# A graph-attention kernel's edge count: target one-hots moved from GpSimd to VectorE, in rings of nine, and the jobs between the counts dealt anew

## Chip, cores and metric

One core of a Trainium2 chip runs the whole program. The metric is the device time of one execution in microseconds (us), the median over the runs shown. Engines: TensorE (PE, its weight loads PEld), VectorE (DVE), ScalarE (ACT), GpSimd (POOL) and SyncE (SP), whose queue issues all DMAs here.

## What is computed

x is [1250, 512] in float32, with 20,000 edges (src, dst), sorted by dst. The reference, cut to what matters:

```python
h = layernorm(x)                                   # no gain
for l in range(2):                                 # 8 heads of 64
    q = (h @ Wq[l].T + bq[l]) * 64 ** -0.5; k = h @ Wk[l].T; v = h @ Wv[l].T
    scores = einsum('ehd,ehd->eh', q[dst], k[src])
    p = softmax of scores over the edges of one dst
    agg = segment_sum(p * v[src], dst)
    h = batchnorm(h + agg @ Wo[l].T + bo[l]) * g1[l] + beta1[l]
    h = batchnorm(h + relu(h @ W1[l].T + b1[l]) @ W2[l].T + b2[l]) * g2[l] + beta2[l]
x = x + layernorm(h) * ln_g + ln_b
x = x + ffn(layernorm(x))                          # nibble decode, three small MLPs, one-hots
```

The kernel computes the attention densely. Two nodes may be joined by several edges, so it needs a matrix of edge counts, count[dst, src]. It adds min(log(count), ...) to each score: the logarithm of the count where there is an edge, and -1e30 where there is none. This 1250 x 1250 matrix is called the bias; it is the same for both layers.

## The kernel before

Nodes are cut into ten tiles of 125 (`NT`, `TILES`). The first block of the program does three things at once, interleaved by hand: the edge count, the layer norm and transposition of the input, and the projections q, v and k of layer 0.

**Edge count.** For each tile j of targets, `counting(j)` on TensorE adds up products of one-hots in three PSUM banks (`counts`, banks 0 to 2): edges come in groups of 125 on the partitions, `onehot_dst[:, k, :]` (125 x 125) marks each edge's target in the tile, `onehot_src[:, k, :]` (125 x 1250) its source. One group takes three matmuls (512, 512 and 226 columns). A loop over registers runs over the groups that touch the tile; a table computed at the start holds first group, number of rounds and rounds before. One round is `RING` = 18 groups; VectorE makes the source one-hots (`step`, L745) into nine slots and the last three target one-hots of each 18, GpSimd makes the other fifteen (`targets`, L596), in steps of three (`STEP`). Then ScalarE computes relu and logarithm of the counts (`logs`), VectorE combines them in a minimum (`combine`, L770), and SP stores the row of the bias (`bias_out`). TensorE may begin the next count only after that minimum, since the banks are the same.

**Gaps.** Between two counts TensorE works through a gap. `GAP_TURNS` and `GAP_REDUCES` say which pairs of tiles of the normed input are transposed there (`turned`: 16 matmuls into two banks of 4 to 7) and split in a high part and a low part (ScalarE copies the high part, `less_high` on TensorE subtracts it, ScalarE copies the rest, `lower`). `JOBS[0]` lists the projection jobs, `GAP_ENDS` where each gap stops in the list, `BANKS[0]` the PSUM bank of each job: transposes of weights ("wq", "wv", "wk", four each; ScalarE and VectorE split them in two parts, `projected` and `reduced`), q and k products (twelve each, of 12 matmuls of up to 418 columns), v products (ten, of 12 matmuls of 512). The order in the list before is wq, q, wv, eight v, wk, two v, k.

```python
GAP_REDUCES = {1: (0, 1), 2: (2, 3), 3: (4,)}
GAP_TURNS = {0: (0, 1), 1: (2, 3), 2: (4,)}
GAP_ENDS = (1, 2, 4, 7, 11, 14, 20, 23, 26, len(JOBS[0]))
```

**Layer norm of the input.** ScalarE sums and squares the rows in two parts, of six and four tiles (`moments`, L632), VectorE finishes the scales after the count of tile 0, ScalarE norms the rows pair by pair. GpSimd adds ln_b to the input (`shift`, L194) for the residual at the very end, in two operations between its target one-hots.

**Keys.** Scores use a high and a low part of k stacked on the partitions, `k_stack`. ScalarE writes the high part to `k_hi`, VectorE the low part to `k_lo` (two buffers each), and `k_stacked` on SP copies both by DMA to where `k_stack` wants them: two DMAs for the high part and two for the low part per chunk c of 128 features. The buffers are reused for chunks 2 and 3. `first_bias` on SP loads the first three tiles of the bias for attention, after k_stacked(0).

The blocks after that: attention of layer 0 (20 passes of four units), output projection and feed-forward, the projections of layer 1 (which use `projected`, `reduced` and `k_stacked` too), attention and feed-forward again, and the final part.

## Time and profile before

| | us |
|---|---|
| runs | 1206.63, 1205.21, 1206.53 (median 1206.53) |
| the profiled execution | 1205.97 |
| its span (first to last instruction) | 1204.2 |
| busy in it: PE / PEld / DVE / ACT / POOL | 1061.8 / 881.6 / 745.8 / 582.0 / 438.1 |
| mean granted TensorE clock | 0.947 of 2.4 GHz |
| first block | 0 to about 299 |
| the ten counts end at | 34.47, 63.26, 92.54, 117.90, 143.60, 163.76, 181.36, 205.42, 224.58, 243.68 |
| last key product of layer 0 ends | 284.12 |
| attention of layer 0 begins | 299.03 |

The profile is of one execution. Busy time of an engine counts its instructions without waiting; a wait has its own column, with the instruction that ended it. PEclk is the clock that TensorE was granted in a stretch, as a share of 2.4 GHz. The counts' ends are the ends of `counting`'s last matmul (L836).

### The profile page before, as it was taken

The page shows a single profiled execution, that of the slowest core. Times are in us where ns is not written, and L with a number is a line of the kernel's source. Part 1 is how long each engine was busy: PE and PEld are TensorE (multiplying, and loading weights), DVE is VectorE, ACT ScalarE, POOL GpSimd, SP SyncE. Part 2 cuts the span into 40 slices and gives each one's busy share as a digit, 9 for nine tenths or more (in the row PEclk, how much of TensorE's full clock was granted, in tenths as well). Part 3 has the DMA queues.
Part 4 walks back from the last instruction along what each step waited for, and adds up shares of the span by engine and source line. Part 5 has one row for each costly group of instructions (what it writes and reads, how often), then busy time and mean ns, then how long its engine had stood idle before and what let it go on. Part 6 is the DMA issues. An engine that isn't in the chain of part 4 may idle for free. (4 is left out here: it accounts for less than half of the span.)

```text
span 1204.2 us, 19750 instructions
## 1 busy us (share of the span) xinstructions
PE 1061.8 (88%) x6706; PEld 881.6 (73%) x6706; DVE 745.8 (62%) x2360; ACT 582.0 (48%) x1085; POOL 438.1 (36%) x519
## 2 busy tenths in 40 slices
PE   3677898995999999999899499989999999989953
PEld 2455676785778888888698499777888888869842
DVE  5434664621767777777577521076777777757788
ACT  5433213231656666666524223365666666652445
POOL 5446665300434444444112100043444444411304
PEclk9878898998999999999999799999999999999985
DMA  6022230139841212123300452484121212321303
GB/s 135 22 90 73 70 114 25 39 71 216 201 101 35 57 35 56 36 47 108 105 1 22 135 117 55 98 193 106 35 56 36 56 35 46 110 79 23 68 2 86
DMA packets 52295, 90.27 MB, mean 75 GB/s; under 512 B 15714, under 2 KB 34014, under 8 KB 51944
## 3 DMA queue, kind: packets, MB, share of 16 engines
q1 hardware_dynamic: 52200, 89.04, 30.1%
q8 instruction: 55, 0.90, 0.3%
q14 instruction: 40, 0.33, 0.1%
HBM read 36.50 MB, written 21.61 MB: 48 GB/s over the span
## 5 line engine op out<-in xcount | busy, mean ns | idle before, releaser
L966 POOL TENSOR_SCALAR probs<-probs,mass_inv 125x1250 f32<-125x1250 f32 x160 | 211.0, 1319 | 359.1 <-DVE mass_inv L1091 359.1
L986 PE MATMUL banks<-k_stack,q_stack 128*125 128x416 f32 (+1 forms) x960 | 299.0, 398 | 19.4 <-DVEq L1069 14.0
L1082 DVE CUSTOM_DVE_ANT_0 probs<-banks,scores_bias 125x416 f32<-125x416 f32 (+1 forms) x480 | 267.3, 582 | 61.0 <-PE banks L986 56.6
L1000 PE MATMUL banks<-ident,probs 125*125 125x125 f32 x1600 | 259.9, 277 | 7.2 <-DVE probs_t L1073 5.2
L1000 PEld LDWEIGHTS banks<-ident,probs 125*125 125x125 f32 x1600 | 242.6, 188 | 30.2 <-issue 22.7
L1052 ACT ACTIVATE probs<-probs,neg_peak 125x1250 f32<-125x1250 f32 x160 | 213.4, 1334 | 53.4 <-DVE neg_peak L1105 53.4
L1041 ACT ACTIVATE probs_t<-banks 125x500 f32<-125x500 f32 x320 | 152.6, 478 | 115.6 <-PE banks L1000 115.4
L1015 PE MATMUL banks<-probs_t,v_pair 125*64 125x250 f32 x1600 | 186.2, 379 | 0.9 <-ACT probs_t L1041 0.9
L986 PEld LDWEIGHTS banks<-k_stack,q_stack 128*125 128x125 f32 x960 | 147.3, 192 | 47.7 <-issue 27.5
L1015 PEld LDWEIGHTS banks<-probs_t,v_pair 125*64 125x64 f32 x1600 | 107.4, 136 | 54.3 <-ACT probs_t L1041 1.3
L1073 DVE COPY probs_t<-banks 125x500 f32<-125x500 f32 x160 | 108.1, 676 | 56.6 <-PE banks L1000 56.6
L831 PE MATMUL banks<-onehot_src,onehot_dst 125*125 125x512 bf16 x540 | 111.1, 370 | 30.9 <-DVE onehot_src L754 24.9
L831 PEld LDWEIGHTS banks<-onehot_src,onehot_dst 125*125 125x125 bf16 x540 | 73.3, 150 | 68.7 <-issue 44.4
L754 DVE TENSOR_SCALAR onehot_src<-iota,e_col 125x1250 bf16<-125x1250 f16 x180 | 94.1, 588 | 38.3 <-PE banks L831 19.5
L611 POOL TENSOR_SCALAR onehot_dst<-own,target_col 125x125 bf16<-125x125 f16 x150 | 104.5, 714 | 10.2 <-POOL target_col L608 10.2
L332 PE MATMUL banks<-h_hi,wt_hi 128*128 128x416 f32 (+1 forms) x192 | 69.6, 362 | 10.0 <-DVE wt_lo L370 10.0
L675 ACT ACTIVATE more<-banks 125x1250 f32<-125x1250 f32 x10 | 12.2, 1216 | 124.0 <-PE banks L836 119.2
L332 PE MATMUL banks<-h_hi,wt_lo 128*128 128x416 f32 (+1 forms) x192 | 68.7, 358 | 0.0
L332 PE MATMUL banks<-h_lo,wt_hi 128*128 128x416 f32 (+1 forms) x192 | 68.7, 358 | 0.0
L1089 DVE TENSOR_SCALAR mass<-mass 125x1 f32<-125x1 f32 x160 | 24.6, 154 | 69.2 <-ACT probs L1052 69.2
L436 POOL CAST q_split<-q_t 128x250 fp32r<-128x250 f32 x40 | 15.8, 396 | 134.7 <-ACT q_t L351 79.1
L1133 POOL TENSOR_TENSOR h_lo<-t,h_hi 128x1250 fp32r<-128x1250 f32 x9 | 25.9, 2874 | 100.8 <-ACT h_hi L1268 100.8
(245 smaller groups left out, 1429.1 us busy)
## 6 DMA issues: line engine op xcount, KB each, us to landing
q_stack<-q_split SPq DMA_DIRECT2D x160, 125.0 KB, 2.3
scores_bias<-edge_bias SPq DMA_DIRECT2D x8, 1171.9 KB
edge_bias<-bias_row SPq DMA_DIRECT2D x10, 585.9 KB
k_stack<-k_hi SPq DMA_DIRECT2D x16, 312.5 KB, 5.4
k_stack<-k_lo SPq DMA_DIRECT2D x16, 312.5 KB, 5.7
resid<-residual SPq DMA_DIRECT2D x2, 2500.0 KB, 9.5
values<-v_stage SPq DMA_DIRECT2D x2, 2400.0 KB
residual<-t SPq DMA_DIRECT2D x4, 625.0 KB, 2.9
```

The costliest lines, as they stand in the source:

```text
L332: mm = nc.tensor.matmul(bank[:, 0:sn], w[:, i, c * P:(c + 1) * P], h[:, i, s0:s0 + sn], **edge)
L611: op = nc.gpsimd.tensor_scalar(onehot_dst[:, k, 0:NT], own[:, 0:NT], target_col[:, k:k + 1], None, ALU.is_equal)
L754: op = nc.vector.tensor_scalar(onehot_src[:, k % SLOTS_SRC, :], iota[:, :], e_col[:, 1, ds(first + RING * q + k, 1)], None, ALU.is_equal)
L831: last = nc.tensor.matmul(counts[:, s:s + w], onehot_dst[:, k, 0:NT], onehot_src[:, k % SLOTS_SRC, s:s + w], start=False, stop=True, skip_ ...
L966: nc.gpsimd.tensor_scalar(probs[:, u % 4, :], probs[:, u % 4, :], mass_inv[:, u % 4:u % 4 + 1], 1.0, ALU.mult, ALU.mult).then_inc(att["pro ...
L986: mm = nc.tensor.matmul(pb[0:NT, t % 5, 0:sn], q_stack[:, n % 2, half, part, tile * NT:(tile + 1) * NT], k_stack[:, head * N + s0:head * N ...
L1000: mm = nc.tensor.transpose(pb[0:NT, 5 + t % 2, j * NT:(j + 1) * NT], probs[:, u % 4, (j0 + j) * NT:(j0 + j + 1) * NT], ident[0:NT, 0:NT])
L1015: mm = nc.tensor.matmul(pb[half * DH:(half + 1) * DH, 7, 0:GN], v_pair[:, c % 2, j, half * DH:(half + 1) * DH], probs_t[:, n % 2, half, j, ...
L1041: nc.scalar.activation(to, of, ACT.Copy).then_inc(att["t_free0"], 1)
L1052: nc.scalar.activation(probs[:, u % 4, :], probs[:, u % 4, :], ACT.Exp, bias=neg_peak[:, u % 4:u % 4 + 1], accum_out=mass[:, u % 4:u % 4 + ...
L1073: nc.vector.tensor_copy(to, of).then_inc(att["t_free1"], 1)
L1082: nc.vector.tensor_tensor_reduce(out=probs[:, slot % 4, s0:s0 + sn], in0=pb[0:NT, t % 5, 0:sn], in1=scores_bias[:, (n % GROUPS) * GROUP + ...
```

## The change

- A round is nine groups (`STEPS` = 3), at least two rounds per tile. VectorE makes all one-hots: per step one operation for three target one-hots and three for source one-hots (`step`). GpSimd's `targets` is gone.
- VectorE makes the first round of a tile before it takes up the minimum of the tile before (`combine(j - 1)`) and the low parts of that gap (`reduces(j - 1)`); the other rounds follow in the loop.
- In tile 0 VectorE waits for all moments of the layer norm between the first round and the loop; one root and one scale operation serve all ten tiles. The input is loaded two tiles at a time.
- `shift` is done by VectorE, in tiles 3 and 4, between minimum and loop.
- ScalarE writes the high part of a key product into `k_stack` itself, in two halves of 64 partitions; VectorE writes the low part in two halves. Only the low part is copied by DMA. This holds for both layers.
- Jobs, gaps and banks are dealt anew: wq, ten q, wv, two q, ten v, wk, twelve k; all k products now come after tile 9's count, all else before it. SP's order follows: wv is loaded before wk, `first_bias` goes out before the last bias row is stored.

```diff
-STEPS = 6
+STEPS = 3
 RING = STEPS * STEP
-SLOTS_SRC = 9
-POOL_STEPS = 5
+LOADS_X = tuple(slice(i, i + 2) for i in range(0, TILES, 2))
...
-        JOBS = (turns("wq") + Q_JOBS + turns("wv") + V_JOBS[0:8] + turns("wk") + V_JOBS[8:] + K_JOBS,
+        Q_FIRST = [("q", c, n) for n in range(3) for c in range(DC)]
+        JOBS = (turns("wq") + Q_FIRST[:10] + turns("wv") + Q_FIRST[10:] + V_JOBS + turns("wk") + K_JOBS,
...
-        GAP_REDUCES = {1: (0, 1), 2: (2, 3), 3: (4,)}
-        GAP_TURNS = {0: (0, 1), 1: (2, 3), 2: (4,)}
-        GAP_ENDS = (1, 2, 4, 7, 11, 14, 20, 23, 26, len(JOBS[0]))
+        GAP_TURNS = {0: (0, 1), 1: (2,), 2: (3,), 3: (4,)}
+        GAP_REDUCES = {1: (0, 1), 2: (2,), 3: (3,), 4: (4,)}
+        GAP_ENDS = (1, 4, 7, 11, 18, 22, 25, 28, 34, len(JOBS[0]))
+
+        LOWER_FIRST = {2: 1, 5: 2, 6: 2, 8: 3, 11: 4}
...
             if job[0] == "k":
                 c, (s0, sn) = job[1], CHUNKS[job[2]]
-                if not job[2] and c >= 2:
-                    act.wait_ge(k_stored[c % 2], 64 * (c // 2))
...
-                nc.scalar.activation(k_hi[c % 2][:, s0:s0 + sn], bank[:, 0:sn], ACT.Copy).then_inc(proj["hi"], 1)
+                for half in range(2):
+                    own, s = slice(half * DH, half * DH + DH), (2 * c + half) * N + s0
+                    op = nc.scalar.activation(k_stack[own, s:s + sn], bank[own, 0:sn], ACT.Copy)
+                op.then_inc(proj["hi"], 1)
...
-                sp.dma_start(f32(k_stack[own, cols]), f32(k_hi[c % 2][own, :])).then_inc(k_stored[c % 2], 16)
                 sp.dma_start(f32(k_stack[other, cols]), f32(k_lo[c % 2][own, :])).then_inc(k_stored[c % 2], 16)
...
-                link(nc.vector.tensor_scalar(span[:, 1, :], span[:, 1, :], 8388608.0, None, ALU.subtract))
+                link(nc.vector.tensor_scalar(span[:, 1, :], span[:, 1, :], 8388608.0, 2.0, ALU.subtract, ALU.max))
...
+                def step(j, first, before, q, i):
+
+                    hold(dve, "dve", onehot_used, RING * (before + q) + STEP * (i + 1))
+                    ks, at_ = range(STEP * i, STEP * (i + 1)), first + RING * q + STEP * i
+                    own = iota[:, j * NT:(j + 1) * NT].rearrange("p (a n) -> p a n", a=1)
+                    targets = e_col[:, 0, ds(at_, STEP)].rearrange("p (k a) -> p k a", a=1)
+                    nc.vector.tensor_tensor(onehot_dst[:, ks.start:ks.stop, 0:NT], own.to_broadcast([NT, STEP, NT]),
+                                            targets.to_broadcast([NT, STEP, NT]), ALU.is_equal)
+                    for k in ks:
+                        op = nc.vector.tensor_scalar(onehot_src[:, k, :], iota[:, :], e_col[:, 1, ds(first + RING * q + k, 1)],
+                                                     None, ALU.is_equal)
+                    op.then_inc(onehots_ready, 1)
...
                 for j in range(TILES):
                     [(first, rounds, before)] = spans_of(dve, j)
-                    with dve.Fori(0, rounds) as q:
-                        for k in range(RING):
-                            step(j, first, before, q, k)
+                    for i in range(STEPS):
+                        step(j, first, before, 0, i)
                     if j == 0:
...
+                        variance()
+                    if j:
+                        combine(j - 1)
+                        reduces(j - 1)
+                    if j == 1:
                         scaled_bias(dve)
...
+                    if j in (3, 4):
+                        dve.wait_ge(shift_in, 16)
+                        dve.wait_ge(h_ready, TILES)
+                        shift(nc.vector, PARTS_X[4 - j]).then_inc(x_shifted, 1)
+                    with dve.Fori(1, rounds) as q:
+                        for i in range(STEPS):
+                            step(j, first, before, q, i)
+                    if j == 0:
+                        scale()
+                combine(TILES - 1)
+                reduces(TILES - 1)
```

`LOWER_FIRST` says which job must wait for which pair's lower copy, `TURN_AFTER` (not shown) which banks a transposition waits for. In `k_stacked` the semaphore counts 32 per chunk instead of 64.

How VectorE's order moves, at the end of tile 1's loop (L779 and L778 are its branches; L370 and L377 the low parts of weights; between L202 or L198 and the next one-hot the table is loaded to registers). Before:

```order
L779 REGISTER_ALU
L779 COMPARE_AND_BRANCH
L773 SCALAR_TENSOR_TENSOR bias_row<-banks,bias_row 125x1250
L370 TENSOR_TENSOR wt_lo_96<-banks,wt_hi_94 128x512
L202 TENSOR_LOAD table
L202 ISA x6
L204 REGISTER_ALU
L204 ISA
L205 ISA x2
L779 UNCONDITIONAL_BRANCH
L779 ISA
L754 ISA
```

After (first lines, and the end of the same round):

```order
L778 REGISTER_ALU
L778 COMPARE_AND_BRANCH
L198 TENSOR_LOAD table
L198 ISA x6
L200 REGISTER_ALU
```

```order
L736 TENSOR_SCALAR onehot_src<-iota,e_col 125x1250
L754 SCALAR_TENSOR_TENSOR bias_row<-banks,bias_row 125x1250
L377 TENSOR_TENSOR wt_lo_94<-banks,wt_hi_92 128x512 x3
L778 UNCONDITIONAL_BRANCH
L778 ISA
L733 ISA
L733 TENSOR_TENSOR onehot_dst<-iota,e_col 125x3x125
```

The minimum of tile 1 stood right behind the loop; now the table's load and nine pairs of one-hots of tile 2 stand ahead of it, and the branch into the loop behind it.

How SP's order moves at the end of the first block (L523 and L529 store a row of the bias, L448 and L454 are `stacked`, L399, L401 and L405, L407 are `first_bias`, L392 and L393 and after the change L399 `k_stacked`). Before, from the last row of the bias on:

```order
L523 DMA edge_bias<-bias_row 120x1250
L523 DMA edge_bias<-bias_row 5x1250
L448 DMA q_stack<-q_split 64x500 x8
L392 DMA k_stack<-k_hi_98 64x1250
L393 DMA k_stack<-k_lo_100 64x1250
L392 DMA k_stack<-k_hi_98 64x1250
L393 DMA k_stack<-k_lo_100 64x1250
L399 DMA scores_bias<-edge_bias 120x2x1250
L399 DMA scores_bias<-edge_bias 5x2x1250
L401 DMA scores_bias<-edge_bias 120x1250
L401 DMA scores_bias<-edge_bias 5x1250
L392 DMA k_stack<-k_hi_99 64x1250
```

After:

```order
L405 DMA scores_bias<-edge_bias 120x2x1250
L405 DMA scores_bias<-edge_bias 5x2x1250
L407 DMA scores_bias<-edge_bias 120x1250
L407 DMA scores_bias<-edge_bias 5x1250
L529 DMA edge_bias<-bias_row 120x1250
L529 DMA edge_bias<-bias_row 5x1250
L454 DMA q_stack<-q_split 64x500 x8
L399 DMA k_stack<-k_lo_96 64x1250 x2
L399 DMA k_stack<-k_lo_97 64x1250 x2
L399 DMA k_stack<-k_lo_96 64x1250 x2
L399 DMA k_stack<-k_lo_97 64x1250 x2
```

The bias load went from behind the first key chunk to ahead of the last bias row, and of sixteen key copies eight are left.

## Rows read from the trace of the kernel before

**Rows 1.** Stretches: us; busy PE, PEld, DVE, ACT, POOL; PEclk, DMA share, GB/s

```profile
34.47:45.96 11.49, 6.69 (x37) 6.55 (x37) 1.46 (x1) 9.46 (x13) 7.45 (x16) 0.70 0.21 57
...
188.15:205.42 17.27, 13.18 (x59) 8.51 (x59) 10.94 (x22) 0.59 (x2) 7.97 (x13) 0.80 0.04 15
...
233.06:243.68 10.62, 10.62 (x60) 7.16 (x59) 5.79 (x13) 0.87 (x2) 0.00 (x0) 1.00 0.01 2
243.68:284.12 40.44, 40.44 (x210) 37.54 (x209) 9.18 (x14) 12.59 (x23) 2.16 (x4) 1.00 0.55 124
284.12:299.03 14.91, 1.48 (x14) 1.12 (x13) 1.59 (x3) 1.47 (x4) 0.00 (x0) 0.71 0.96 211
```

**Rows 2.** Lines, 0 to 250 us: busy us, mean ns | idle before, releasers

```profile
L831 PE MATMUL banks<-onehot_src,onehot_dst 125*125 125x512 bf16 x540 | 111.1, 370 | 30.9 <-DVE onehot_src L754 24.9 <-POOL onehot_dst L611 6.0
...
L754 DVE TENSOR_SCALAR onehot_src<-iota,e_col 125x1250 bf16<-125x1250 f16 x180 | 94.1, 588 | 38.3 <-PE banks L831 19.5 <-issue 18.0
...
L773 DVE SCALAR_TENSOR_TENSOR bias_row<-banks,bias_row 125x1250 f32<-125x1250 f32 x10 | 14.6, 1459 | 53.6 <-ACT bias_row L679 53.6
...
L752 DVE TENSOR_TENSOR onehot_dst<-iota,e_col 125x375 bf16<-125x375 f16 x10 | 6.0, 603 | 0.3
```

**Rows 3.** Timeline (start us, us, engine, line) of PE, tiles 7 and 9

```profile
192.97 12.31 PE L831 MATMUL banks<-onehot_src,onehot_dst 125*125 125x512 bf16 x54 [4.08 <-DVE onehot_src L754]
...
233.73 9.81 PE L831 MATMUL banks<-onehot_src,onehot_dst 125*125 125x512 bf16 x54
```

**Rows 4.** Timeline, all engines, the end of the first block

```profile
292.13 1.34 ACT L346 ACTIVATE k_hi<-banks 128x418 fp32r<-128x418 f32 x3 [14.19 <-DMA k_stack<-k_lo]
292.68 1.59 DVE L367 TENSOR_TENSOR k_lo<-banks,k_hi 128x418 fp32r<-128x418 f32 x3 [14.12 <-ACT k_hi L346]
294.30 0.46 SPq L392 DMA_DIRECT2D k_stack<-k_hi  x1
...
297.11 1.00 SPq L393 DMA_DIRECT2D k_stack<-k_lo  x1
...
299.03 1.38 PE L986 MATMUL banks<-k_stack,q_stack 128*125 128x418 f32 x3 [13.43 <-DVEq L1069]
```

**Rows 5.** Timeline of DVE, first one-hots of tiles 2, 4 and 5

```profile
78.25 4.19 DVE L754 TENSOR_SCALAR onehot_src<-iota,e_col 125x1250 bf16<-125x1250 f16 x9 [3.13 <-issue]
...
123.57 6.15 DVE L754 TENSOR_SCALAR onehot_src<-iota,e_col 125x1250 bf16<-125x1250 f16 x1 [1.45 <-issue]
...
148.85 4.19 DVE L754 TENSOR_SCALAR onehot_src<-iota,e_col 125x1250 bf16<-125x1250 f16 x9 [1.13 <-issue]
```

**Rows 6.** Timeline of ScalarE at the start

```profile
13.85 0.63 ACT L637 ACTIVATE ln_scratch<-xs 125x512 f32<-125x512 f32 x1 [11.79 <-DMA xs<-in_x]
...
27.91 1.28 ACT L649 ACT_TABLE_LOAD   x1
```

**Rows 7.** Timeline of PE, pieces of the gaps

```profile
63.19 1.20 PE L858 MATMUL banks<-h_hi,minus_ident 128*128 128x250 f32 x8
...
66.89 5.46 PE L847 MATMUL banks<-ident,h_norm 125*128 125x125 f32 x32 [2.49 <-ACT h_lo L669]
...
227.39 0.39 PE L329 MATMUL banks<-wt_hi,h_hi 128*125 128x512 f32 x1
...
230.19 0.40 PE L329 MATMUL banks<-wt_hi,h_hi 128*125 128x512 f32 x1
...
249.30 1.91 PE L317 MATMUL banks<-ident,wk_nat 128*128 128x128 f32 x16
```

**Rows 8.** Line 1133 on VectorE: x count: ns min/median/max

```profile
L1133 DVE TENSOR_TENSOR h_lo<-t,h_hi x6: 803/806/810, 637.8 to 1120.5; 128x625 fp32r<-128x625 f32 x6
```

**Rows 9.** Timeline of POOL, tile 1 to tile 2

```profile
68.95 0.29 POOL L602 COPY own<-iota 125x125 f16 x1 [0.93 <-POOL onehot_dst L611]
```

**Rows 10.** Timeline of PE, first scores of pass 3, layers 0 and 1

```profile
339.96 0.65 PE L986 MATMUL banks<-k_stack,q_stack 128*125 128x418 f32 x2 [2.81 <-DMA q_stack<-q_split]
...
821.92 0.65 PE L986 MATMUL banks<-k_stack,q_stack 128*125 128x418 f32 x2 [2.50 <-DMA q_stack<-q_split]
```

More of the change, by code:

```diff
@@ L171, in gnn_ffn @@
         wk_in = sem("wk_in")
-        x_in = [sem("x_in0"), sem("x_in1")]
+        x_in = [sem(f"x_in{k}") for k in range(len(LOADS_X))]
         e_in, consts, e_float, e_turned, hits_ready, hits_turned = (sem(s) for s in (
@@ L355, in projected @@
                     act.wait_ge(res_stored, 16 * DC)
+                    if layer == 0:
+                        for k in range(2):
+                            act.wait_ge(shifted_stored[k], 32)
                 nc.scalar.activation(v_pair[:, :, job[1], :], bank[0:NT, 0:4 * DH].rearrange("p (c d) -> p c d", c=2), ACT.Copy)
@@ L366, in reduced @@
                 c, (s0, sn) = job[1], CHUNKS[job[2]]
-                op = nc.vector.tensor_tensor(k_lo[c % 2][:, s0:s0 + sn], bank[:, 0:sn], f32(k_hi[c % 2][:, s0:s0 + sn]), ALU.subtract)
+                if not job[2] and c >= 2:
+                    dve.wait_ge(k_stored[c % 2], 32 * (c // 2))
+                if not job[2] and layer == 0 and c < 2:
+                    for k in range(2):
+                        dve.wait_ge(bias_stored[k], 32 * (TILES // 2))
+                for half in range(2):
+                    own, s = slice(half * DH, half * DH + DH), (2 * c + half) * N + s0
+                    op = nc.vector.tensor_tensor(k_lo[c % 2][own, s0:s0 + sn], bank[own, 0:sn], f32(k_stack[own, s:s + sn]), ALU.subtract)
             else:
@@ L511, in _ @@
                 xv = x.rearrange("(t p) d -> p t d", p=NT)
-                for k, tiles in enumerate(PARTS_X):
+                for k, tiles in enumerate(LOADS_X):
                     for rows in SPREAD:
@@ L548, in _ @@
                 shifted(0)
[L549 to L552 removed]
+                turned_out("wv")
+                sp.dma_start(w_nat[0]["wk"][:, :, :], weight(gnn["Wk"], DC)[:, 0:DC, :]).then_inc(wk_in, 16)
+                for j in range(5, TILES - 1):
                     bias_out(j)
```

149 lines of the change are left out of this document (49 added, 100 removed).

## Prediction, made before the changed kernel ran

> **What bounds the kernel now.** On the page TensorE leads every other engine in busy time, so I looked for the stretches in which it idles or runs slowly. The table of stretches, cut at the beginning and end of each tile's count, gives them [rows 1]: a count that runs undisturbed takes 10.62 us (tile 9), the one of tile 7 takes 17.27 us at a mean clock of 0.80, the gap after tile 0 takes 11.49 us, and at the end of the block 14.91 us pass with 1.48 us of matmuls. The groups by line say what TensorE waits for in the counts [rows 2]: 24.9 us on source one-hots of VectorE, 6.0 us on target one-hots of GpSimd. VectorE meanwhile sat idle 53.6 us in front of its minimum with the logarithm (L773). The timeline of TensorE shows one such wait [rows 3]: in tile 7 the 54 matmuls start after 4.08 us of idling and take 12.31 us; in tile 9, started warm, they take 9.81. So a late first one-hot costs twice, in waiting and in half clock (1.2 of 2.4 GHz) behind it. At the end of the block [rows 4], ScalarE's copies of the keys' high parts waited 14.19 us for a DMA of the low parts to free the buffer, at a DMA share of 0.96 [rows 1]; SP issued its last copy at 297.11 and attention began at 299.03, 14.9 us behind the last projection matmul (284.12).
>
> **The change, part by part.** I build TensorE's time anew, from T, the end of a count.
> *One-hots.* GpSimd's part goes; VectorE makes six groups of three target one-hots per tile where it made one. Nine source one-hots take 4.19 us [rows 5], 0.465 from start to start where one alone lasts 588 ns; a group of three target one-hots lasts 603 ns [rows 2], by the same ratio 0.47. A step of three pairs is 3 x 0.465 + 0.47 = 1.87 us, nine pairs 5.6, a tile 11.2. TensorE uses three in 9.81 / 6 = 1.6 us. With nine ready when the count begins, TensorE has 4.9 us of work, and the second nine come in time if VectorE enters its loop by then.
> *The order.* VectorE's last one-hot of a tile ends about 2 us before T (TensorE still has the last three, 1.6), then 1.1 to 3.1 us pass in loading the table and entering (1.13 and 3.13 [rows 5]; 18.0 over ten tiles [rows 2]), nine pairs 5.6, the minimum 1.46: the bias row is ready at T - 2 + 1.7 + 5.6 + 1.5 = T + 6.8, where it used to follow the logarithm at once. TensorE's next count stands behind it, and that is hidden while a gap lasts over 6.8 us.
> *Layer norm of the input and tile 0.* ScalarE's sums began at 13.85 on the load of six tiles and its squares ended about 27.8, right ahead of the table load at 27.91 [rows 6]. With two-tile loads only the last two tiles of the first part wait for the full 13.85: 4 x 0.62 = 2.5 us earlier. But VectorE now waits for all of it between its first and second nine of tile 0: 25.3 + 0.2 + 0.9 to enter the loop + 5.6 = 32.0, and TensorE, idle for some 5.5 us once its first nine are used, does the last three by 33.8 at full clock or 35.3 at half. Before, tile 0 ended at 34.47 [rows 1]; I take 34.5, no gain. Which clock? The row that is nearest in length is the 4.08 us of idling in tile 7, which cost 2.5 us [rows 3]. The Trainium skill, TensorE: Matmul & The Clock Gate, What's actually happening, says that throttled is the default and activity releases it. By that rule it is 35.3 and 0.8 us more in all; the trace agrees where it can be read, with the clock of 0.80 in tile 7's count.
> *Gaps.* Prices [rows 7]: a v product 230.19 - 227.39 = 2.80 us, a weight's transpose 1.91 / 4 = 0.48; a k or q product from the gap after tile 9, which is four v, four transposes and twelve k in 40.44 us [rows 1], (40.44 - 11.2 - 1.9) / 12 = 2.28; the transposes of a pair of tiles 5.46 / 2 = 2.7, less_high of a pair 0.6; where a transpose needs a lower copy first, it begins at T + 3.6 (66.89 - 63.26). Gap 0 stays 11.5. Gap 1: 3.6 + 2.7 + 1.5 = 7.8. Gap 2: 0.6 + 2.7 + 3 products = 10.1. Gap 3: 0.6 + 2.7 + 4 products = 12.4. Gap 4: wait to 3.7 (bank 4 needs the last lower copy), 3 products, 4 transposes = 12.4. Gap 5: 2 q + 2 v = 10.1. Gaps 6 and 7: 8.4 each. Gap 8: 2 v + 4 transposes = 7.5. Sum of 1 to 8: 77.1. All exceed 6.8, the last one barely.
> *Stalls left.* Tile 1: VectorE's loop starts after the minimum and a weight's low part, 0.8. Tile 3: the shift waits for the last normed rows (I estimate 2.4 us into the count: a copy and two activations of ScalarE), runs, and only then the second nine come: 1.7. The shift itself: 806 ns for 625 elements [rows 8] gives at most 2.64 us for 2,048 and 3.96 for 3,072; the second is hidden in gap 3. The Trainium skill, VectorE: DVE Perf Modes, The TRN2 errata, has (N + 151) / 0.96 ns for such an add, 2.29 us for 2,048, which would make 1.7 into 1.4; for 625 it gives 808 ns, and the trace agrees with 806. With the shift off GpSimd goes its effect too: in tile 4 VectorE's first one-hot took 6.15 us beside it [rows 5].
> *Branch.* Each count now runs its loop body twice, so TensorE takes a backward branch that the trace of before never shows for it. Bounds: 0, since matmuls queued ahead cover it, and 0.93 us, GpSimd's idling at its own outer branch with a table load [rows 9]. I take 0.2 x 10 = 2.0, nearer to the covered end, for TensorE's forward branch is not visible at all.
> *Sum.* 34.5 + 11.5 + 9 x 10.62 + 2.5 + 77.1 + 12 x 2.28 + 2.0 = 250.5 for the end of the last key product (before 284.12).
> *Keys in place.* ScalarE and VectorE each do two half operations per product, about 0.9 + 1.1 us (1.34 / 3 and 1.59 / 3 each [rows 4]) under a product of 2.28: hidden, except behind the last. Half of the 16 key copies (312.5 KB each) go, and the first bias load now goes out during tile 9's count, so that no buffer is awaited. Then 2.0 + two issues of some 0.5 (0.46 at 294.30) + 0.9 to the next block (as 298.11 to 299.03): attention starts 4.0 us behind, at 254.5. The bias row of tile 9, the q stacks and four bank cycles lie in front of the key copies, but end some 13 us into 27 us of products.
> *After that* nothing is gained: the stall on q_stack was 2.81 us in layer 0 and 2.50 in layer 1 [rows 10], where the key copies had long landed, so it comes from bias and v traffic, which stays. Layer 1's projections keep TensorE full, so its halved copies gain nothing either.
> Total: 299.03 - 254.5 = 44.5 us. The profiled execution took 1205.97; that gives 1161.5, and against the median of 1206.53, 0.56 higher, 1162.
>
> **The rivals.**
> (a) *VectorE paces the tiles.* If both idlings (table, loop entry) are 3.1 us and one-hots take 0.54 as with some contention, the second nine begin to arrive at T - 1.4 + 3.1 + 6.8 + 1.5 + 3.1 + 2.3 = T + 15.4, where TensorE wants them at gap + 0.8 + 4.9, T + 13.2 to 14.1, and then at 2.3 us a step against 1.6: about 3.5 us in each of five tiles with short gaps, 17 in all: 1179. For it: VectorE's work per tile rises to some 15 us in one chain. Against: before, it kept pace with GpSimd contending.
> (b) *Better than forecast.* Branch free, tile 1 and 3 unstalled, x early enough for tile 0 to end at 33.5, the q_stack stall gone with the backlog: 2.0 + 2.5 + 1.0 + 2.8 = 8 us: 1154.
> (c) *The tail's stall stays*, since the low copies queue behind the bias loads: 10.8 us back, 1173. Against: half the bytes, and the bias load goes first by 20 us.
> (d) *Slower.* TensorE's backward branch in the middle of each count costs as much as VectorE's longest idling ahead of a first one-hot, 3.13 us [rows 5], with no matmul queued to cover it, and each such idling brings half clock behind it, 2.5 us as in tile 7 [rows 3]: 5.6 us a tile, 56 in ten, less the 2.0 that I have: 1216. It decides from (44.5 + 2.0) / 10 = 4.65 us a tile. Against: VectorE's idlings hold a table load too, GpSimd's own branch with one took 0.93 [rows 9], and TensorE entered its loops without a visible stop.
> (e) *The change doesn't do what it says*: a third round in a tile would add matmuls. 540 matmuls are 10 x 18 x 3 [rows 2], one round of 18 in every tile, so two rounds of nine are exactly as many. Excluded.
>
> **How the numbers follow.** Forecast 0.70, (a) 0.15, (b) 0.07, (c) 0.04, no gain at all 0.01, (d) 0.03. The forecast's own terms range over: branch 0 to 9.3 (+7.3), half clock behind the waits of gaps 1 and 4 (up to 2.5 each), tile 0 up to 2.5 later; not all together, 1154 to 1176. Taking in most of (b) and (c) and leaving out (d) and the worse half of (a): 1152 to 1178. A measurement of this kernel can tell 0.2% from no change: faster 0.96, same 0.01, slower 0.03.
>
> **What the new profile would show.** Counts of 10.6 to 11 us from tile 2 on, tile 3 near 12.3; one-hots at 0.465 us; no wait of TensorE on one-hots over 2 us but in tile 0; the minimum ending about 6.8 us after each count; the last key product ending near 250, attention starting some 4 us later, and no DMA wait on k_lo. Wrong would be: waits of the count's first matmuls on the bias row in every tile, waits in the middle of each count without a semaphore (the branch), or an end of the block beyond 270.

## The result, and the profile of the changed kernel

The changed kernel takes 1161.6 us (median of 4 runs, 1160.4 to 1162.6), the kernel before 1206.6 in the same session (4 runs, 1205.2 to 1208.1): a ratio of 0.963, 95% interval 0.961 to 0.964. The forecast was 1162.0. The last key product ends at 250.62 (forecast 250.5), attention starts at 255.12 (254.5), where before it started at 299.03 [rows 4]. From there on nothing was gained or lost that can be told: 905.7 us to the end of the span against 905.2. That remainder was 905.2 to 909.2 in the fourteen profiles of this study, which hides differences of a few us between medians; where an experiment acts on the first block, the start of attention is the sharper measure, and both are given.

Busy time on the page (busy, share of the span):

```profile
PE 1052.4 (91%) x6706; PEld 875.8 (75%) x6706; DVE 776.3 (67%) x2429; ACT 594.1 (51%) x1108; POOL 306.8 (26%) x306
```

VectorE took 30 us more and GpSimd 131 less than before. The groups by line, 0 to 260 us (no count runs after 223; busy us, mean ns, idle before), answer to [rows 2]:

```profile
L821 PE MATMUL banks<-onehot_src,onehot_dst 125*125 125x512 bf16 x540 | 103.4, 350 | 2.9 <-DVE onehot_src L736 2.7
...
L736 DVE TENSOR_SCALAR onehot_src<-iota,e_col 125x1250 bf16<-125x1250 f16 x180 | 87.3, 545 | 0.0
...
L733 DVE TENSOR_TENSOR onehot_dst<-iota,e_col 125x375 bf16<-125x375 f16 x60 | 32.9, 549 | 42.9 <-PE banks L821 38.0 <-issue 4.9
L754 DVE SCALAR_TENSOR_TENSOR bias_row<-banks,bias_row 125x1250 f32<-125x1250 f32 x10 | 14.6, 1458 | 4.9 <-ACT bias_row L662 4.9
```

TensorE's idling ahead of count matmuls fell from 30.9 to 2.9 us. VectorE waits for TensorE now (38.0 us, for free slots), and no more for the logarithm but in the last tile (4.9 of 53.6).

The stretches (us; busy PE, PEld, DVE, ACT, POOL; clock, DMA share, GB/s): gap 0, gap 4, count 5, count 8, twelve k products, end of the block:

```profile
31.57:44.38 12.81, 7.18 (x37) 6.96 (x37) 6.93 (x13) 10.36 (x15) 0.00 (x0) 0.73 0.18 49
117.68:133.61 15.93, 10.85 (x58) 10.21 (x57) 7.67 (x14) 7.28 (x11) 0.00 (x0) 0.89 0.51 137
133.61:145.89 12.28, 12.28 (x59) 8.05 (x59) 7.42 (x16) 0.00 (x0) 0.00 (x0) 0.86 0.23 86
194.40:205.02 10.62, 10.62 (x60) 7.16 (x59) 7.36 (x16) 0.87 (x2) 0.00 (x0) 1.00 0.02 5
223.07:250.62 27.55, 27.55 (x144) 26.93 (x144) 14.26 (x23) 13.73 (x24) 1.03 (x2) 1.00 0.59 145
250.62:255.12 4.50, 1.49 (x14) 1.13 (x13) 1.36 (x3) 1.16 (x3) 0.00 (x0) 0.89 0.23 49
```

The last line answers to the 14.91 us at a DMA share of 0.96 of [rows 1]. Gap 4 and the count behind it are the dear ones, and gap 0, at a clock of 0.73. The timeline (start, us, engine, line; idling in brackets) of the places that matter, in order of time:

```profile
6.98 0.63 ACT L620 ACTIVATE ln_scratch<-xs 125x512 f32<-125x512 f32 x1 [4.98 <-DMA xs<-in_x]
...
26.00 5.44 PE L821 MATMUL banks<-onehot_src,onehot_dst 125*125 125x512 bf16 x27 [1.60 <-DVE onehot_src L736]
...
36.38 6.73 PE L839 MATMUL banks<-ident,h_norm 125*128 125x125 f32 x32 [4.80 <-ACT h_norm L638]
...
59.13 1.45 DVE L754 SCALAR_TENSOR_TENSOR bias_row<-banks,bias_row 125x1250 f32<-125x1250 f32 x1
...
85.69 2.29 DVE L194 TENSOR_TENSOR xs<-xs,shift_all 125x2048 f32<-125x2048 f32 x1 [6.31 <-ACT h_norm L638]
...
100.21 3.36 DVE L194 TENSOR_TENSOR xs<-xs,shift_all 125x3072 f32<-125x3072 f32 x1
...
121.40 0.69 PE L331 MATMUL banks<-h_hi,wt_hi 128*128 128x416 f32 x1 [3.06 <-ACT h_lo L652]
...
133.61 0.73 PE L814 MATMUL banks<-minus_one,one_row 1*125 1x512 bf16 x3 [2.02 <-issue]
...
255.12 6.31 PE L978 MATMUL banks<-k_stack,q_stack 128*125 128x418 f32 x18 [3.01 <-DVEq L1061]
```

Counts 1 to 9 start at 44.38, 63.58, 83.89, 107.06, 133.61, 156.17, 175.27, 194.40 and 212.45; counts 0 to 9 end at 31.57, 55.01, 74.20, 95.54, 117.68, 145.89, 166.79, 185.89, 205.02 and 223.07. From these come the stretches used below. Every profile is of one execution, and some stretches differ between profiles although the edit leaves them alone: the end of tile 0 stood at 31.4 to 33.2 us in nine of them, gap 1 took 7.0 to 8.6 us without idle matmuls, and count 5 took 10.62 or 12.28. A difference of some 2 us in the start of attention can be no more than that.

### The profile page after: what moved, and what is told of

It is laid out like the page before. It is cut to its first block and busy times, and to the rows that moved or that the text cites. A ratio compares the mean times of both kernels' runs of the same rounds, so it can differ in the third digit from the quotient of the medians.

```text
span 1160.8 us, 19123 instructions
## 1 busy us (share of the span) xinstructions
PE 1052.4 (91%) x6706; PEld 875.8 (75%) x6706; DVE 776.3 (67%) x2429; ACT 594.1 (51%) x1108; POOL 306.8 (26%) x306
## 5 line engine op out<-in xcount | busy, mean ns | idle before, releaser
L1044 ACT ACTIVATE probs<-probs,neg_peak 125x1250 f32<-125x1250 f32 x160 | 213.4, 1334 | 53.7 <-DVE neg_peak L1097 53.6
L821 PE MATMUL banks<-onehot_src,onehot_dst 125*125 125x512 bf16 x540 | 103.4, 350 | 2.9 <-DVE onehot_src L736 2.7
L821 PEld LDWEIGHTS banks<-onehot_src,onehot_dst 125*125 125x125 bf16 x540 | 68.5, 141 | 37.4 <-issue 11.0
L736 DVE TENSOR_SCALAR onehot_src<-iota,e_col 125x1250 bf16<-125x1250 f16 x180 | 87.3, 545 | 0.0
L733 DVE TENSOR_TENSOR onehot_dst<-iota,e_col 125x375 bf16<-125x375 f16 x60 | 32.9, 549 | 42.9 <-PE banks L821 38.0
## 6 DMA issues: line engine op xcount, KB each, us to landing
resid<-residual SPq DMA_DIRECT2D x2, 2500.0 KB, 10.1
```

The costliest lines, as they stand in the source:

```text
L733: nc.vector.tensor_tensor(onehot_dst[:, ks.start:ks.stop, 0:NT], own.to_broadcast([NT, STEP, NT]), targets.to_broadcast([NT, STEP, NT]), A ...
L736: op = nc.vector.tensor_scalar(onehot_src[:, k, :], iota[:, :], e_col[:, 1, ds(first + RING * q + k, 1)], None, ALU.is_equal)
L821: last = nc.tensor.matmul(counts[:, s:s + w], onehot_dst[:, k, 0:NT], onehot_src[:, k, s:s + w], start=False, stop=True, skip_group_check= ...
L1044: nc.scalar.activation(probs[:, u % 4, :], probs[:, u % 4, :], ACT.Exp, bias=neg_peak[:, u % 4:u % 4 + 1], accum_out=mass[:, u % 4:u % 4 + ...
```

## Experiments

**1. Keys by DMA again.** In the changed kernel only this is undone, in both layers (the two high buffers, the waits for them and SP's copies of them, cut here, come back with it):

```diff
-                for half in range(2):
-                    own, s = slice(half * DH, half * DH + DH), (2 * c + half) * N + s0
-                    op = nc.scalar.activation(k_stack[own, s:s + sn], bank[own, 0:sn], ACT.Copy)
-                op.then_inc(proj["hi"], 1)
...
+                nc.scalar.activation(k_hi[c % 2][:, s0:s0 + sn], bank[:, 0:sn], ACT.Copy).then_inc(proj["hi"], 1)
...
+                sp.dma_start(f32(k_stack[own, cols]), f32(k_hi[c % 2][own, :])).then_inc(k_stored[c % 2], 16)
```

> The changed kernel (1161.6 us) with one part undone: the keys' high parts go through two buffers and DMAs again, with the waits that the kernel before had for them (ScalarE before chunk 2, SP at the end of both blocks); the order of jobs, the one-hots and the early bias load stay as changed. Theory A (the tail's gain has two sources: half the key copies and no buffer to wait for, and the bias load moved ahead of all key copies): the high copy of chunk 2 waits for chunk 0's four DMAs, which start only behind the q stacks (about 237 us in), so some 2 to 4 us of TensorE's pauses come back, and SP issues 8 more copies (0.5 to 2 us each) ahead of the next block: attention starts 3 to 7 us later than 255.1, total 1165 to 1169, expected 1167. Theory B (keys in place is the whole gain of the tail): attention starts 14.9 us behind the last key product again, total about 1172 or more. Theory C (the order of the bias load is the whole gain): within 1.5 us of the changed kernel.

Measured: 1166.0 us (1162.9 to 1170.5). Its timeline at the end of the block:

```profile
246.40 1.34 ACT L346 ACTIVATE k_hi<-banks 128x418 fp32r<-128x418 f32 x3 [8.04 <-DMA k_stack<-k_lo]
...
256.46 1.62 SPq L396 DMA_DIRECT2D k_stack<-k_lo  x1
...
260.13 6.09 PE L977 MATMUL banks<-k_stack,q_stack 128*125 128x418 f32 x18 [7.21 <-DVEq L1060]
```

The last key product ended at 251.44, so 8.7 us pass to the start of attention, where the changed kernel has 4.5; attention starts 5.0 us later in all. Theory A holds, in one detail not as told: ScalarE waited 8.04 us for the copies, but TensorE's products took 27.55 us as before, without a pause. The price comes only at the end, from copies that SP issues late (its last at 256.46).

**2. The bias load behind the key copies.** The changed kernel with SP's old order:

```diff
-                first_bias(sp)
...
                 bias_out(TILES - 1)
                 for n in range(2):
                     stacked(sp, n)
-                for c in range(DC):
+                k_stacked(sp, 0, 0)
+                sp.wait_ge(proj["copied"], len(V_JOBS) + len(Q_JOBS))
...
+                first_bias(sp)
+                for c in range(1, DC):
                     k_stacked(sp, 0, c)
```

> The changed kernel with SP's old order at the end of the block: the first bias load (four DMAs, 1.9 MB) stands behind the last bias row, the q stacks and the key copies of chunk 0, so it goes out near 239 us instead of 214; keys stay in place. Theory A (two sources of the tail's gain): the copies of chunks 1 to 3 land behind these 1.9 MB, VectorE's low part of chunk 3 waits some 4 us for its buffer and the end of the block moves by 2 to 4 us: expected 1164, range 1163 to 1166. In the kernel before with keys in place the attention started 7.2 us behind the last key product, 2.7 more than the 4.5 here. Theory B (keys in place is the whole gain): 1161 to 1162.3. Theory C (the order is nearly the whole): 1168 or more.

Measured: 1168.3 us (1163.6 to 1172.1), 11.4 us between last product (248.36) and attention, which starts 4.7 us later than in the changed kernel.

```profile
236.28 2.14 SPq L405 DMA_DIRECT2D scores_bias<-edge_bias  x2
...
254.09 3.64 DVE L374 TENSOR_TENSOR k_lo<-banks,k_stack 64x418 fp32r<-64x418 f32 x6 [10.16 <-DMA k_stack<-k_lo]
```

The mechanism is theory A's, but I had priced the wait at 4 us and it is 10.16: the copies of chunk 1 go out behind 1.9 MB and hold the buffer of chunk 3. In size it is theory C's case, above theory A's range.

**3. Keys in place alone**, in the kernel before (the inverse of the first diff, one-hots, jobs and SP's order as they were).

> The kernel before (1206.5 us) with one part of the change alone: the keys' high parts are written in place by ScalarE in two halves, only the low parts are copied by DMA, in both layers. One-hots, jobs and SP's order stay as before (the bias load behind the key copies of chunk 0). Theory A (two sources, see the other experiment): ScalarE waits no more, VectorE's low parts of chunks 2 and 3 still wait for copies that stand behind the first bias load; attention starts 5 to 9 us earlier than at 299.0: 1198 to 1202, expected 1199. Theory B (keys in place is all of the tail's gain, 10.4 us): 1196. Theory C (the order is all): 1205 to 1207.

Measured: 1197.1 us (1195.4 to 1198.8), ratio to before 0.9925 (0.990 to 0.995).

```profile
283.12 3.64 DVE L371 TENSOR_TENSOR k_lo<-banks,k_stack 64x418 fp32r<-64x418 f32 x6 [5.93 <-DMA k_stack<-k_lo]
...
288.82 2.42 PE L989 MATMUL banks<-k_stack,q_stack 128*125 128x418 f32 x6 [5.71 <-DVEq L1072]
```

By the total this misses theory A's range (1198 to 1202) and stands nearer to B's 1196. The stretch itself says otherwise: 7.2 us from the last product (281.62) to attention, against 14.9, so in place alone gives 7.7 of the 10.4 us. The other 2.5 us came before the last product, where the edit touches nothing until the key products (the longest piece is count 2, 18.07 us against 19.82). With experiments 1 and 2: 14.9 with neither, 8.7 with the order alone, 7.2 or 11.4 with keys in place alone (in the kernel before, in the changed one), 4.5 with both. No single edit is the whole gain of the tail, so theory B falls, by experiments 1 and 2 above all. The two also save partly the same time.

**4. VectorE not ahead.** The changed kernel, with the minimum and the low parts in front of the first round:

```diff
+                    if j:
+                        combine(j - 1)
+                        reduces(j - 1)
                     for i in range(STEPS):
                         step(j, first, before, 0, i)
                     if j == 0:
                         variance()
-                    if j:
-                        combine(j - 1)
-                        reduces(j - 1)
```

> The changed kernel with one part undone: VectorE takes up the minimum and the low parts of the gap before the first round of one-hots, instead of after it. All else stays, also that VectorE makes all one-hots. Theory A (being ahead is what removes the waits): the bias row comes 1.4 us earlier, which nobody waits for, but in the gaps with weight transposes (0, 1, 4 and 8) VectorE can begin one-hots only when the last low part is written, about 2 us behind the gap's end, so those counts begin 2 to 3 us late and then go at VectorE's pace (1.83 us a step against 1.6) at half clock for a while, 3 to 5 us each, 12 to 20 in all; in the other tiles the nine are ready or nearly. Expected 1176, range 1171 to 1183. Theory B (it was GpSimd's slow target one-hots alone, the order of VectorE's work is worth nothing): 1160 to 1164.

Measured: 1179.1 us (1177.3 to 1180.9), attention at 271.13, 16.0 later. The count matmuls by line, then stretches (counts 1, 2, 4, 5 and 9):

```profile
L821 PE MATMUL banks<-onehot_src,onehot_dst 125*125 125x512 bf16 x540 | 109.2, 364 | 15.1 <-DVE onehot_src L736 14.9
```

```profile
42.38:58.28 15.90, 12.32 (x59) 8.04 (x59) 11.71 (x26) 3.01 (x6) 0.00 (x0) 0.89 0.01 2
65.32:81.97 16.65, 12.75 (x59) 8.32 (x59) 13.03 (x27) 3.11 (x6) 0.00 (x0) 0.79 0.32 102
...
115.39:126.01 10.62, 10.62 (x59) 7.16 (x59) 6.35 (x13) 0.14 (x1) 0.00 (x0) 1.00 0.09 32
141.56:156.72 15.16, 12.33 (x59) 8.04 (x59) 12.60 (x27) 0.54 (x2) 0.00 (x0) 0.89 0.19 71
224.62:239.08 14.46, 12.32 (x59) 8.04 (x59) 11.90 (x26) 0.00 (x0) 0.07 (x1) 0.88 0.63 130
```

The counts behind gaps with weight transposes (0, 1, 4 and 8) grew, by 2.9 to 6.0 us; count 3 grew by 0.4, and the others, as count 4, kept their 10.62. That is 18.4 us, of which the gaps gave 2.3 back. Undoing the order alone costs 16.0 us by the start of attention, 17.5 by the medians. Theory B falls.

**5. The shift on GpSimd.** The changed kernel, with

```diff
+                pool.wait_ge(shift_in, 16)
+                pool.wait_ge(h_ready, TILES)
+                for k in (1, 0):
+                    shift(nc.gpsimd, PARTS_X[k]).then_inc(x_shifted, 1)
```

in place of VectorE's two shifts.

> The changed kernel with the shift back on GpSimd, both operations one behind the other as soon as the last rows are normed (about 85.7 us in). Before, GpSimd took 4.54 us for 2048 elements and 6.73 for 3072. VectorE saves 2.29 us in tile 3 and 3.36 in tile 4. Theory A (a VectorE one-hot cannot go on beside the shift, as the one of 6.15 us in tile 4 of before): the shifts lie on VectorE's second nine of tile 3, which are blocked until 90 or until 97; TensorE has used its first nine at 89.6 and waits 1 to 8 us, with half clock behind it. Expected plus 6, 1165 to 1173. Theory B (no blocking to speak of): tile 3's stall of 0.4 us and its late half clock go, 1160 to 1162.

Measured: 1173.5 us (1172.8 to 1174.5), just above theory A's range; attention at 264.48, 9.4 later.

```profile
85.61 11.42 POOL L194 TENSOR_TENSOR xs<-xs,shift_all 125x2048 f32<-125x2048 f32 x2 [80.37 <-ACT h_norm L642]
86.94 3.58 DVE L737 TENSOR_TENSOR onehot_dst<-iota,e_col 125x375 bf16<-125x375 f16 x1 [7.69 <-PE banks L821]
90.44 7.83 DVE L740 TENSOR_SCALAR onehot_src<-iota,e_col 125x1250 bf16<-125x1250 f16 x3
...
98.42 7.66 PE L821 MATMUL banks<-onehot_src,onehot_dst 125*125 125x512 bf16 x27 [9.00 <-DVE onehot_src L740]
```

VectorE's target one-hots, 0.55 us alone, ended at 90.52, about when the first shift must have ended (85.61 + 4.54), and its next three operations (1.45 us alone) took 7.83 across the second, which ended at 97.03. TensorE waited 9.00 us and went at half clock behind it. The Trainium skill, SBUF — State Buffer, Who interferes with whom, calls the pair of ports that both engines share an exclusive lock, held for a whole instruction; the trace agrees, with both kinds of one-hots. Theory A holds, under-priced: count 3 took 22.48 us instead of 11.65, 10.8 more, and 1.7 came back in count 5, which took 10.62 here as in other runs that leave it alone.

**6. The input in two loads** (the changed kernel, `LOADS_X = PARTS_X`).

> The changed kernel with the input loaded in two parts of six and four tiles again, instead of five of two. Tile 0 ended at 31.57 us (31.4 to 33.2 in the runs so far), 2.9 earlier than in the sum and than before, since ScalarE's sums began near 8 us and its squares ended at 23.3. Theory A (the small loads are the cause): the sums begin at 13.85 and the squares end at 27.9 as before; VectorE waits for them between its first and second nine, so tile 0 ends 4.5 us later, at 36, and all else follows: 1166, range 1164.5 to 1167.5. Theory B (x simply lands earlier in the changed program): 1161 to 1162.5.

Measured: 1168.1 us (1166.6 to 1171.2); tile 0 ends at 38.78, attention starts at 259.00.

```profile
14.21 0.63 ACT L620 ACTIVATE ln_scratch<-xs 125x512 f32<-125x512 f32 x1 [12.21 <-DMA xs<-in_x]
...
30.87 7.77 PE L821 MATMUL banks<-onehot_src,onehot_dst 125*125 125x512 bf16 x27 [6.04 <-DVE onehot_src L736]
```

The total lies above theory A's range (1164.5 to 1167.5). Tile 0 ends 7.2 us later, where 4.5 were expected: the wait inside the count is 6.04 us, and the 27 matmuls behind it take 7.77 against 5.44. Of these, 3.3 came back before attention (gap 0 took 10.83, count 5 10.62, and the latter has nothing to do with the loads), so the loads are worth 3.9 to 5.5 us by attention's start and 6.5 by the medians. They are no ornament of this change: VectorE now waits for the moments in the middle of tile 0, and only they make that cheap.

**7. Gap 4 dealt again** (job 11 to bank 6, wv's transposes behind it, two q products last):

```diff
-        JOBS = (turns("wq") + Q_FIRST[:10] + turns("wv") + Q_FIRST[10:] + V_JOBS + turns("wk") + K_JOBS,
+        JOBS = (turns("wq") + Q_FIRST[:8] + turns("wv") + Q_FIRST[8:] + V_JOBS + turns("wk") + K_JOBS,
...
-        LOWER_FIRST = {2: 1, 5: 2, 6: 2, 8: 3, 11: 4}
+        LOWER_FIRST = {2: 1, 5: 2, 6: 2, 8: 3, 14: 4}
```

> The changed kernel with gap 4 dealt again: its first q product goes to bank 6, which no transposed rows occupy, instead of bank 4; wv's four transposes follow it, and two q products come last in the gap instead of the transposes. In the changed kernel this gap took 15.93 us where the sum had 12.4 (TensorE waited 3.06 us for the last low copy of h, worked at half clock until 124.5, and idled 2.02 us behind the transposes with nothing shown that it waited for), and the count behind it 12.28 us at clock 0.86 where an undisturbed one takes 10.62. Theory A (bank 4 is the cause, and the short transposes at the gap's end leave the register load that opens the next count uncovered): gap 4 is 0.7 + 3 x 2.28 + 1.9 = 9.5 us, count 5 is 10.6: 8.0 us less, 1153.6, range 1152 to 1156. Theory B (only the wait goes, the idling and the slower count have another cause): 3 to 4.5 us less, 1157 to 1159.

Measured: 1157.6 us (1155.1 to 1160.3); attention at 250.59, 4.5 earlier. Its ratio to before, 0.959 (0.957 to 0.961), just overlaps that of the changed kernel; the gap itself took 11.37 us instead of 15.93. Theory B: the 3.06 us wait is gone, the 2.03 us of idling (127.03 to 129.06) and the slow count (12.29) stayed. What TensorE's sequencer did in that gap, in the changed kernel, then here (counts, ns min/median/max, start):

```profile
L198 PEldq TENSOR_LOAD <-table x1: 2906/2906/2906, 129.3 to 129.3; - x1
```

```profile
L198 PEldq TENSOR_LOAD <-table x1: 4074/4074/4074, 123.6 to 123.6; - x1
```

It reads the tile's three entries of the table. That read took 0.76 us in gap 8 of the changed kernel (762 ns at 210.2, DMA share 0.00), 2.91 in its gap 4 (DMA share 0.76 meanwhile) and 4.07 here (0.91). 1.1 us of register work follow, and the matmuls queued ahead run out.

**8. The table read early** (the changed kernel, TensorE's ten reads replaced by two of five tiles each, ahead of the first count):

```diff
+                spans = [s for j in range(0, TILES, 5) for s in spans_of(pe, j, 5)]
...
-                    [(first, rounds, before)] = spans_of(pe, j)
+                    first, rounds, before = spans[j]
```

> The changed kernel with one thing moved: TensorE reads all ten tiles' entries of the table into registers before the first count (two reads of 15 values), instead of three values in each gap. In the changed kernel this read on TensorE's sequencer took from 0.76 us (gaps 1, 6, 7, 8, where no large DMA ran) to 2.5 to 2.9 us (gaps 0, 2, 4, 5), 4.07 in the run with gap 4 dealt again, and 1.1 us of register work follow it; TensorE idled 0.84, 0.35 and 2.02 us ahead of counts 1, 3 and 5. Theory A (the read beside DMA traffic is that idling, and the slow count 5 its half clock): these 3.2 us go and count 5 returns from 12.28 to 10.62: 4.9 less, 1156.7, range 1155 to 1159. Theory B (the idling is something else, as loading of code): 1160.5 to 1162.5.

Measured: 1171.3 us (1168.2 to 1174.6). As a version it is a miss, as a test a hit. Register work on 30 values kept the first count back from 14.9 to 31.22, tile 0 ended at 44.43. But from there to attention it took 218.1 us, against 223.6 in the changed kernel: 5.4 less, where 4.9 were expected. Gap 4 and count 5:

```profile
128.83:142.70 13.87, 10.81 (x58) 10.24 (x57) 5.70 (x11) 6.36 (x10) 0.00 (x0) 0.88 0.51 143
142.70:153.32 10.62, 10.62 (x60) 7.16 (x59) 9.29 (x20) 0.91 (x2) 0.00 (x0) 1.00 0.35 116
```

So the late read caused the idling of 2.02 us and with it the half clock of count 5, 3.7 us together (the rest is gap 0, 1.7 shorter). The other runs that deal gap 4 as the changed kernel does bear the idling out: where this read took 1.20, 1.92, 1.92, 2.10, 2.17, 2.71, 2.78 and 2.91 us, TensorE idled 0.31, 1.03, 1.03, 1.22, 1.31, 1.82, 1.93 and 2.02 us behind it. Count 5 took 10.62 to 10.63 us behind the waits of 1.03 to 1.31 and 12.27 to 12.28 behind the three longest; so these 3.7 us can be 1.0 in another execution. That the DMA traffic makes the read slow is only seen together with it, not shown apart.

**9. Rows normed before the logarithm** in gap 0 (ScalarE's `normed` of the first two pairs put ahead of `logs(0)`).

> The changed kernel with one thing moved: in gap 0 ScalarE norms the first four tiles of rows before it computes relu and logarithm of tile 0's count, instead of after. Gap 0 took 12.81 us where the sum had 11.5; TensorE waited 4.80 us in it for the first normed row, while ScalarE had idled 6.78 us ahead of the relu and the scales were ready at 30.65, 0.9 us before the count's end. Theory A: the transposes start at about 31.7 instead of 36.4 and take 6.7; the first minimum ends near 39.9 as before, since VectorE's first nine of tile 1 stand ahead of it until 38.36; count 1 starts near 40 instead of 44.4: 4.4 us less, 1157.2, range 1156 to 1158.5. Theory B (the bias row of tile 0 is now late: the logarithm starts 2 us later, and VectorE's first round is not the longer path): 2 us less or nothing, 1159 to 1162.

Measured: 1160.5 us (1154.9 to 1164.6). Gap 0 and count 1:

```profile
33.08:40.16 7.08, 4.21 (x36) 3.97 (x36) 6.93 (x13) 7.05 (x11) 0.00 (x0) 1.00 0.00 0
40.16:54.08 13.92, 13.92 (x59) 8.82 (x59) 7.79 (x17) 3.26 (x6) 0.00 (x0) 0.75 0.17 47
```

The gap gave 5.7 us, and 3.3 went in the count behind it, which TensorE began after idling 2.88 us for the bias row; it was busy without a pause, at a clock of 0.75. Attention started at 252.72, 2.4 us earlier, but 1.7 of them are count 5. The interval overlaps that of the changed kernel: no gain that can be told. Theory B has the size and half of the reason: the bias row was late, but the greater loss is clock.

**10. Clock kept.** Experiment 9 with 18 matmuls that compute nothing (`keep_clock(3, 18)`) in gap 0.

> The kernel of the experiment in which ScalarE norms first in gap 0, with 18 idle matmuls of TensorE (bf16, 256 columns, into bank 3, which nothing holds then) between the transposed rows and wq's transposes. There the gap went from 12.81 to 7.08 us, but TensorE idled 2.88 us in it for the bias row and count 1 took 13.92 us at a mean clock of 0.75 instead of 10.63. Theory A (count 1's loss is half clock behind that idling and nothing else): with 18 x 0.12 = 2.2 us of the idling filled, count 1 takes 10.6 to 11.2: 3.0 less than that kernel, so about 4.1 + 1.4 (its tile 0 ended 1.5 later) = some 5.5 less than the changed one at the best: 1157, range 1156 to 1158.5. Theory B (VectorE paces count 1 there, since the bias row and the first round stand in one chain): 1159.5 to 1161.

Measured: 1161.4 us (1160.2 to 1164.6). Gap 0, count 1, gap 1:

```profile
32.03:40.33 8.30, 6.22 (x55) 5.80 (x55) 6.93 (x13) 8.27 (x12) 0.00 (x0) 1.00 0.01 3
40.33:52.61 12.28, 12.28 (x59) 8.12 (x59) 7.78 (x17) 3.25 (x6) 0.00 (x0) 0.86 0.19 52
52.61:62.51 9.90, 7.41 (x38) 6.88 (x37) 6.34 (x13) 7.58 (x12) 0.00 (x0) 0.66 0.00 0
```

Count 1 got back 1.6 of 3.3 us, not all, and gap 1 lost them again (9.90 against 8.40 in experiment 9, at a clock of 0.66). Neither theory: VectorE did not pace the count, which ran without a pause. That the matmuls only moved the half clock is not shown apart, but the only other kernel with them, experiment 12, has 9.89 us in gap 1 too, and no form of the changed kernel without them more than 8.6.

**11. Three together** (experiments 7 and 9, and both shifts one tile later).

> The changed kernel with both of these and the two shifts one tile later (in tiles 4 and 5; before, VectorE waited 6.31 us for the last normed rows ahead of the shift of tile 3, and TensorE's second nine of that tile came 0.4 us late with half clock behind them, 11.65 us against 10.62). If the three are independent: 1161.6 - 8.0 - 4.4 - 1.0 = 1148.2, range 1146 to 1151. If the time came back later (bias row too late in the shortened gap 4, or the stall on q_stack growing): 1152 or more.

Measured: 1154.5 us (1151.0 to 1162.2), ratio to before 0.958 (0.955 to 0.961), attention at 247.79. It is the fastest version found, 6 to 7 us ahead of the changed kernel (0.963, 0.961 to 0.964), but 6 short of the sum. Part came back: count 1 took 13.24 us (13.92 in experiment 9), and with the shift stored a tile later the read of gap 5 took 4.20 us, TensorE idled 1.23 behind it and count 6 took 12.28.

**12. All, with early reads and the clock kept.**

> All of it together: gap 4 dealt again, normed first, the shifts a tile later, the early reads of the table and the idle matmuls in gap 0. In the run with the first three the attention started at 247.8; in it count 1 took 13.24 us (2.3 too much), TensorE idled 0.35, 1.96 and 1.23 us ahead of counts 3, 5 and 6, and count 6 took 12.28 (1.7 too much). Taken off: 7.5 us from 1154.5, 1147, range 1144 to 1150. If the idling comes back as a wait for the bias row in the shortened gaps: 1150 to 1153.

Measured: 1164.3 us (1162.0 to 1165.5): a miss by experiment 8's late start (tile 0 ended at 44.71). From there to attention it took 212.0 us, 11.5 less than in the changed kernel. What it would be with a cheap early read was not tried.

## Why the forecast held, and where it did not

The mechanism was as told, and the total came out within 0.4 us, but partly because errors cancel: in this table the terms above their forecast add up to 5.7 us, those below to 5.2.

| term | forecast | profile |
|---|---|---|
| end of tile 0 | 34.5 | 31.57 |
| gap 0 | 11.5 | 12.81 |
| nine counts with their stalls | 98.1 | 98.28 |
| gaps 1 to 3, 5 to 8 | 64.7 | 64.48 |
| gap 4 | 12.4 | 15.93 |
| backward branch | 2.0 | 0 |
| twelve k products | 27.4 | 27.55 |
| last product to attention | 4.0 | 4.50 |

- *Tile 0.* The step that failed was that the first part's last tiles would wait for the full 13.85 us. Sums began at 6.98, those tiles' at 11.78, squares ended at 23.4 instead of 25.3, and TensorE waited 1.60 us in the count, not 5.5. Experiment 6 shows that the small loads are the cause, worth 5.6 to 7.4 us there (38.78 against 31.4 to 33.2). "No gain" was wrong by 2.9.
- *Gap 0.* I kept 11.5; it was 12.81 at a clock of 0.73, with 0.84 of idling ahead of the count, which experiment 8 puts down to the table's read.
- *Counts.* Full ones took 10.62 (10.63 in tile 1, 11.65 in tile 3). VectorE's step took 1.83 us, not 1.87. Tile 1 did not stall (forecast 0.8), tile 3 lost 1.0 (1.7), all of it VectorE's pace, for the clock stayed at 1.00. The shifts took 2.29 and 3.36 us, the first exactly the Trainium skill's figure (VectorE: DVE Perf Modes, The TRN2 errata); that, and a start 1.80 us into the count instead of 2.4, made the stall smaller than mine. The 1.7 us of count 5 were not in the sum: half clock behind the late read.
- *Other gaps.* Their row hides such errors too: gap 1 took 8.57 us (forecast 7.8), gap 2 9.69 (10.1), gap 3 11.52 (12.4). The transposes of a pair were priced at 2.7 us from a row that stood behind a wait; in gap 2, without one and at a clock of 1.00, they took 1.71 (74.70 to 76.41), in gap 1, behind 2.50 us of waiting, 2.75.
- *Gap 4.* The wait for bank 4 was priced (until 3.7 us into the gap; it was 3.72), the half clock behind it was put in the range, and the 2.02 us of the read were nowhere. Experiments 7 and 8 name both.
- *Bias row.* In tile 1 it stood at T + 5.6, not T + 6.8 (60.58 against 55.01), in tiles 2 to 8 at T + 4.8 to 5.6. The step that was off is the entry: VectorE began its next nine 1.4 to 2.2 us before the count ended, at most 0.9 us behind its last one-hot, where I had 1.7 us and 0.3 before the end. The shortest gap is 7.43 us, hence no count waited for the row.
- *Branch.* Nothing. The counts with a backward branch take the 10.62 us that tile 9 took without one [rows 1].
- *End of the block.* 4.50 against 4.0; experiments 1 to 3 bear out that both parts, keys in place and the early bias load, are needed. One sign did not come as told: VectorE's low parts did wait for DMAs, 4.60 us for the bias row's store (225.73 + 1.46 to 231.79) and 2.97 for a buffer:

```profile
242.26 2.42 DVE L374 TENSOR_TENSOR k_lo<-banks,k_stack 64x418 fp32r<-64x418 f32 x4 [2.97 <-DMA k_stack<-k_lo]
```

  TensorE's products went on over both, 27.55 us without a pause.
- *Attention.* The stall on the q stacks stayed, as forecast (2.98 us in layer 0, 3.70 in layer 1).
- *Rivals.* VectorE as the pacer (a) needed one-hots at 0.54; they came at 0.46, with GpSimd idle. (b) had the branch, tile 1 and tile 0 right, not tile 3 and the q stacks, and gaps 0 and 4 with count 5 took back 6.5 us of it. (c) in part is what experiment 2 makes of the kernel (6.9 of its 10.8 us). (d) falls with the branch.
- *What was not taken apart.* Attention starts 43.9 us earlier. The experiments price the tail (10.4 us), VectorE's order (16.0) and the loads (3.9 to 5.5). The rest, some 12 to 14 us if these add up, is shared by the target one-hots' move to VectorE, the rings of nine, the shift's place and the new order of jobs. No run undoes the move, the rings or the order of jobs alone, so it is not shown what the move in itself is worth.

## What to carry to other kernels

Here a wait of TensorE could cost twice, as idling and as half clock behind it (2.02 and 1.7 us at count 5); shortening a gap down to a bare wait gave 5.7 us and lost 3.3 in the count behind it, and empty matmuls in the wait gave back 1.6 of these and no time in all. Where an engine serves a consumer and also waits for slower ones, let it first make what the consumer needs next and then take up the wait: here that order was worth 16 of 44 us. Before moving work between engines, ask what shares a port or a queue with it: one shift on GpSimd cost 11.9 us, one bias load ahead of small copies 6.7.
